# Attention block with residual and layernorm: the softmax reciprocals spread through DRAM, the division taken from PSUM, and a new order of all engines

## The chip, the cores and the metric

The kernel runs on one core of one Trainium2 chip. The metric is the device time in microseconds (us) of the whole launch, all 32 batches in one program; lower is better.

## The reference

`x` is 32 x 256 x 384 (32 batches, 256 rows, 384 columns), `adj` 32 x 256 x 256, all in float32; there are 12 heads of 32 columns.

```python
q, k = x @ Wq.T, x @ Wk.T                      # per head: [32, 12, 256, 32]
v = x @ Wv.T + bv
a = einsum('bnhd,bmhd->bhnm', q, k) * SCALE + adj[:, None]     # [32, 12, 256, 256]
a = where(all(a == 0, axis=-1)[..., None], -inf, a)
a = nan_to_num(softmax(a, axis=-1))            # a row that was all zero gives zero
o = einsum('bhnm,bmhd->bnhd', a, v)            # back to [32, 256, 384]
out = layernorm(x + o @ Wo.T + bo)             # over the 384 columns, eps 1e-5
```

## The kernel before, in words

**Work.** The batches go through a software pipeline, and each of the five instruction streams (TensorE, VectorE, ScalarE, GpSimd and the DMA queue of SyncE) has its own order, written out by hand as a list of calls: `start()` for the first batches, `step(t)` for batches 3 to 29, `end()` for the last. Semaphores alone tie the streams together. A step of TensorE holds work of four batches: `nxt2` (t+2), `nxt` (t+1), `prev` (t-1), `prev2` (t-2).

**A batch.** TensorE projects k and q in three pieces K01, K2Q0 and Q12 (`project_kq`, 18 matmuls each, every float32 product made from three products of split halves `_hi` and `_lo`) into bank_c or bank_b. It projects v in two halves (`project_v`, 9 matmuls each, bank_b). `scores(t, g)` makes the scores of four heads (group g, 0 to 2) in four banks `s_bank`, 24 matmuls. VectorE's `add_bias` adds adj, negates and takes the row's extreme, one instruction per head and half of the rows: 24 in a batch, in 12 units of two. ScalarE's `exps` takes the exponential of a unit and leaves the row sums in `sums`. The unnormalised weights must be transposed. For groups 0 and 1 VectorE transposes them in 32x32 blocks (`square`, 8 in a batch), SyncE stores 1 MB to DRAM (`store_squares`, sq_dram) and loads it in another order (`load_squares`, sq_probT). For group 2, units 8 to 11, TensorE transposes (`transposes`, 4 matmuls a unit, into bank_t) and ScalarE copies out (`copy_probT`). `weigh(t, g)` multiplies v by the weights, 16 matmuls into bank_a, which holds one group at a time, transposed (columns of o on the partitions).

**Division, which the change touches.** `invert` (L1264, VectorE) makes the 24 reciprocals of each row. They stand with rows on the partitions, but the weighed values have rows along the free axis. So GpSimd widens them 32 times (`widen_inv`, L418), and TensorE transposes the wide tile with six matmuls (`spread`, L858), four into bank_c (R0) and two into bank_t (R1). Meanwhile ScalarE copies each weighed group out of bank_a (`save_o`, L576, into o_raw), which frees the bank for the next `weigh`. VectorE multiplies o_raw by the bank of reciprocals (`divide`, L1273, once for groups 0 and 1, once for 2) into o_n, one buffer. `split_o_hi` (ScalarE) and `split_o_lo` (GpSimd) split o_n; `project_y` (9 matmuls each of two halves) applies Wo; VectorE's `residual` and `moments`, GpSimd's `deviation` and ScalarE's `normalise` finish the batch.

**The flag.** `find_zero`, `flag` (one matmul, into the free half of bank_a), `read_flag` (L1240) and `mask` look for rows that are all zero. `mask` loads the flag into a register of VectorE's sequencer (L1248) and branches over its body.

**What may wait.** `weigh` waits until the bank was saved, `scores(t, g)` until `add_bias` has read the four banks of the group before it, and the DMA queue issues strictly in its order, so a wait at its head holds back everything behind it:

```python
def load_squares(t, g):
    sp.wait_ge(sq_stored[g], t.count(DMA, DMA))
    apart(sp)
    after(sp, pv_done[g], t.count(1))
```

Of the kernel before, what the change touches and what calls it, by code (L numbers as in the profile page):

```python
# [13 lines left out]
P = 128  # L14
# [66 lines left out]
def build(nc, x, xT, adj, wqT, wkT, wvT, bv, woT, bo, out):  # L81
    def sb(name, shape, dt=F32):
# [23 lines left out]
    sums = [sb(f"sums{p}", [P, NT, H]) for p in range(2)]  # L106
# [15 lines left out]
    most = sb("most", [P, NT, H])  # L122
    inv = sb("inv", [P, NT, H])
    inv_wide = sb("inv_wide", [P, NT, H, HD])
    o_raw = [sb(f"o_raw{p}", [P, KC, N]) for p in range(2)]
    o_n = sb("o_n", [P, KC, N])
# [19 lines left out]
    bank = {"R0": bank_c, "K01": bank_c, "Q12": bank_c, "PV0": bank_a, "PV1": bank_a, "PV2": bank_a,  # L146
            "K2Q0": bank_b, "V0": bank_b, "V1": bank_b, "Y0": bank_b, "Y1": bank_b}
    t_flat = bank_t[:].rearrange("p k m q -> p (k m q)")
    bank["R1"] = t_flat
    flags_at = bank_a[:, N:N + NT * H]  # L150
# [3 lines left out]
    last_bank = {"R0": s_flat[0], "Y0": s_flat[0], "R1": s_flat[1], "Y1": s_flat[1], "PV1": s_flat[2], "PV2": bank_c[:]}  # L154
# [42 lines left out]
    o_saved = [sem(f"o_saved{g}") for g in range(KC)]  # L197
# [4 lines left out]
    inv_wide_ready = sem("inv_wide_ready")  # L202
    inv_spread = sem("inv_spread")
# [11 lines left out]
    CONSTS = 4  # L215
# [7 lines left out]
    with nc.Block() as block:  # L223

        @block.sync
        def _(sp):
# [32 lines left out]

            def store_out(t):  # L260
# [27 lines left out]
            def start():  # L288
                t0 = Batch(0)
                t1 = Batch(1)  # L290
                t2 = Batch(2)
                t3 = Batch(3)
                t4 = Batch(4)
                load_bias(t1)
                load_xt(t2)
                load_xr(t0)
                store_squares(t0, 0)
                load_xr(t1)
                load_squares(t0, 0)
                load_xt(t3)  # L300
                store_squares(t0, 1)
                load_xt(t4)
                load_squares(t0, 1)
                load_bias(t2)
                store_squares(t1, 0)
                store_squares(t1, 1)
                load_squares(t1, 0)
                load_squares(t1, 1)
                load_bias(t3)
                store_squares(t2, 0)  # L310
                load_squares(t2, 0)
                load_xr(t2)
                store_squares(t2, 1)
                load_bias(t4)
                load_squares(t2, 1)
                store_squares(t3, 0)
                store_out(t0)

            def step(t):
                nxt2 = t.later(2)  # L320
                nxt = t.later(1)
                prev2 = t.later(-2)
                load_xt(nxt2)
                load_bias(nxt2)
                load_squares(t, 0)
                store_squares(t, 1)
                load_squares(t, 1)
                load_xr(t)
                store_squares(nxt, 0)
                store_out(prev2)  # L330

            def end():
                t28 = Batch(28)
                t29 = Batch(29)
                t30 = Batch(30)
                t31 = Batch(31)
                store_squares(t30, 1)
                load_squares(t30, 0)
                load_squares(t30, 1)
                store_squares(t31, 0)  # L340
                load_xr(t30)
                load_squares(t31, 0)
                store_squares(t31, 1)
                store_out(t28)
                load_squares(t31, 1)
                store_out(t29)
# [5 lines left out]
            for c in range(3, 30):  # L352
                step(Batch(c))
# [4 lines left out]
        def _(pool):  # L358
# [3 lines left out]
            pool.wait_ge(const_ready, 3)  # L362
# [41 lines left out]
            def split_o_lo(t, k):  # L404
# [5 lines left out]
                nc.gpsimd.tensor_tensor(o_lo[:, a:b], o_n[:, a:b], o_hi[:, a:b].bitcast(F32), ALU.subtract  # L410
                                        ).then_inc(o_ready, 1)

            def widen_inv(t):
                pool.wait_ge(inv_ready, t.count(1, 1))

                after(pool, inv_spread, t.count(2))
                apart(pool)
                nc.gpsimd.tensor_copy(inv_wide[:], inv[:].unsqueeze(3).to_broadcast([P, NT, H, HD])  # L418
                                      ).then_inc(inv_wide_ready, 1)
# [19 lines left out]
            def start():  # L439
# [9 lines left out]
                split_kq(t0, "Q12")  # L449
                permute_bias(t1)  # L450
                split_kq(t1, "K01")
                split_xt(t2)
                split_kq(t1, "K2Q0")
                split_kq(t1, "Q12")
                split_kq(t2, "K01")
                widen_inv(t0)
                split_kq(t2, "K2Q0")
                split_kq(t2, "Q12")
                permute_bias(t2)
                split_xt(t3)  # L460
                add_bo(t0)
                split_xt(t4)
                split_o_lo(t0, 0)
                split_kq(t3, "K01")
                split_o_lo(t0, 1)
                widen_inv(t1)
                split_kq(t3, "K2Q0")
                permute_bias(t3)
                add_bo(t1)
                split_kq(t3, "Q12")  # L470
                deviation(t0)
                widen_inv(t2)
                split_o_lo(t1, 0)
                split_kq(t4, "K2Q0")

            def step(t):
# [4 lines left out]
                permute_bias(nxt)  # L481
                split_o_lo(prev2, 1)
                split_kq(nxt, "K01")
                add_bo(prev)
                split_xt(nxt2)
                split_kq(nxt, "Q12")
                deviation(prev2)
                split_kq(nxt2, "K2Q0")
# [1066 lines left out]
```

## Time and profile before

| | |
|---|---|
| median of 3 runs | 718.36 us (717.56 to 718.78) |
| profiled execution, its own time | 718.51 us |
| its span, first to last instruction | 716.2 us |
| outside the span | 2.3 us |
| mean granted TensorE clock | 0.997 |

The profile page gives each engine's busy time, the span in 40 slices, and the chain of work that ended last. From its trace come groups of instructions by line, the same chain in order of time, and the instructions of a stretch with what each waited for. A steady batch begins every 21.45 us (K01 at 317.44 and at 338.89).

### The profile page before, as it was taken

What the parts mean: (1) busy time and instruction counts of PE and PEld (TensorE: products, weight loads), DVE (VectorE), ACT (ScalarE), POOL (GpSimd) and SP (SyncE); (2) the same over time, 40 slices, a digit from 0 to 9 for tenths busy, and PEclk for the clock granted to TensorE, in tenths of its full rate; (3) what the DMA queues carried; (4) which work ended last, traced back from release to release, by engine and by line L of the source; (5) the groups of instructions that cost most, each with busy time, mean ns of one, the idle gap of its engine ahead of it and who ended that gap; (6) DMA issues with size and microseconds to landing.
All of it is one profiled execution on the core that took longest, in us unless ns stands there. A gap on an engine that the chain in (4) does not pass through costs nothing.

```text
span 716.2 us, 23143 instructions
## 1 busy us (share of the span) xinstructions
PE 698.7 (98%) x7557; PEld 600.7 (84%) x7557; DVE 600.1 (84%) x2220; ACT 613.8 (86%) x1993; POOL 487.2 (68%) x548
## 2 busy tenths in 40 slices
PE   8999999999999999999999999999999999999895
PEld 8878888888888888888888888888898888888774
DVE  4898988889888889888889888889888889888973
ACT  4889988889988889988888988889888888898882
POOL 4767666677766678766677766678766677766452
PEclk9999999999999999999999999999999999999998
DMA  8475877787777687777787777787777777777672
GB/s 266 152 278 206 300 267 264 252 315 236 263 263 273 241 309 240 265 264 267 251 302 240 262 267 259 252 305 247 257 270 261 262 291 248 255 273 259 248 288 90
DMA packets 84008, 184.61 MB, mean 258 GB/s; under 512 B 4272, under 2 KB 42928, under 8 KB 75696
## 3 DMA queue, kind: packets, MB, share of 16 engines
q1 hardware_dynamic: 83888, 183.12, 72.3%
q8 instruction: 61, 1.00, 0.6%
q14 instruction: 59, 0.48, 0.2%
HBM read 103.42 MB, written 79.69 MB: 256 GB/s over the span
## 4 chain that ended last, share of the span: by engine, by line
PE 85%; DVE 5%; DMA 4%; issue 2%; POOL 2%; ACT 1%; SPq 0%; DVEq 0%; ACTq 0%; POOLq 0%
PE bank_b L787 34%; PE bank_c L787 16%; PE bank_a L877 12%; PE s_bank L836 11%; PE bank_t L847 8%; PE bank_c L858 2%; DVE neg L1192 2%; DMA sq_dram<-w_f 2%; DMA sq_probT<-sq_dram 2%; ACT prob L559 1%; PE bank_t L858 1%; DVE w_f L1209 1%; DMA xt<-in_xT 1%; POOL kq_lo L400 0%; DVE y L1292 0%
## 5 line engine op out<-in xcount | busy, mean ns | idle before, releaser
L559 ACT ACTIVATE prob<-neg,negmax 128x256 f32<-128x256 f32 x768 | 380.3, 500 | 51.8 <-DVE w_f L1209 34.3
L1192 DVE CUSTOM_DVE_ANT_0 neg<-s_bank,bias_sq 128x256 f32<-128x256 f32 x512 | 185.2, 414 | 49.0 <-issue 42.6
L1209 DVE STREAM_TRANSPOSE w_f<-prob 128x512 f32<-128x512 f32 x256 | 173.2, 696 | 0.7 <-ACT prob L559 0.7
L559 ACT ACTIVATION_READ_ACCUMULATOR prob<-neg,negmax 128x1 f32 x768 | 147.7, 192 | 0.0
L400 POOL TENSOR_TENSOR kq_lo<-kq,kq_hi 128x512 fp32r<-128x512 f32 x96 | 125.2, 1304 | 7.7
L398 POOL CAST kq_hi<-kq 128x512 fp32r<-128x512 f32 x96 | 60.2, 627 | 79.3 <-issue 73.9
L787 PE MATMUL bank_c<-xt_hi,w_hi 128*128 128x256 f32 x384 | 111.1, 289 | 1.0 <-DVE w_lo L1171 1.0
L787 PE MATMUL bank_c<-xt_hi,w_lo 128*128 128x256 f32 x384 | 108.3, 282 | 0.0
L787 PE MATMUL bank_c<-xt_lo,w_hi 128*128 128x256 f32 x384 | 108.3, 282 | 0.0
L1192 DVE CUSTOM_DVE_ANT_0 neg<-s_bank,bias 128x256 f32<-128x256 f32 x256 | 91.0, 420 | 15.2 <-PE s_bank L836 15.0
L847 PE MATMUL bank_t<-ident,prob 128*128 128x128 f32 x512 | 80.3, 279 | 0.7 <-ACT probT L569 0.7
L569 ACT ACTIVATE probT<-bank_t 128x512 f32<-128x512 f32 x128 | 75.0, 586 | 3.6 <-PE bank_t L847 2.9
L787 PEld LDWEIGHTS bank_c<-xt_hi,w_hi 128*128 128x128 f32 x384 | 73.0, 190 | 2.1 <-issue 1.7
L410 POOL TENSOR_TENSOR o_lo<-o_n,o_hi 128x512 fp32r<-128x512 f32 (+1 forms) x62 | 63.4, 1025 | 15.4 <-ACT o_hi L584 15.4
L787 PEld LDWEIGHTS bank_c<-xt_hi,w_lo 128*128 128x128 f32 x384 | 73.1, 190 | 0.0
L787 PEld LDWEIGHTS bank_c<-xt_lo,w_hi 128*128 128x128 f32 x384 | 73.1, 190 | 0.0
L877 PE MATMUL bank_a<-sq_probT,v 128*32 128x256 f32 x1008 | 67.5, 385 | 1.2 <-DVE zero_flag L1240 1.0
L787 PE MATMUL bank_b<-w_hi,o_hi 128*128 128x384 f32 x186 | 68.3, 367 | 0.3 <-DVE y L1292 0.3
L787 PE MATMUL bank_b<-w_hi,xt_hi 128*128 128x384 f32 x192 | 67.8, 353 | 0.3 <-ACT kq L542 0.2
L836 PE MATMUL s_bank<-kq_hi 32*128 32x256 f32 x768 | 65.2, 328 | 2.6 <-POOL kq_lo L400 1.3
L836 PEld LDWEIGHTS s_bank<-kq_hi 32*128 32x128 f32 x768 | 37.3, 183 | 34.4 <-issue 33.3
L847 PEld LDWEIGHTS bank_t<-ident,prob 128*128 128x128 f32 x512 | 56.5, 140 | 10.7 <-issue 1.6
(88 smaller groups left out, 1794.1 us busy)
## 6 DMA issues: line engine op xcount, KB each, us to landing
sq_dram<-w_f SPq DMA_DIRECT2D x64, 1024.0 KB, 4.5
sq_probT<-sq_dram SPq DMA_DIRECT2D x64, 1024.0 KB, 5.6
xt<-in_xT SPq DMA_DIRECT2D x32, 384.0 KB, 4.5
xr<-in_x SPq DMA_DIRECT2D x32, 384.0 KB, 6.2
out_y<-y_out SPq DMA_DIRECT2D x31, 384.0 KB, 3.0
bias<-in_adj SPq DMA_DIRECT2D x32, 256.0 KB, 3.2
w_f<-in_wkT SPq DMA_DIRECT2D x3, 192.0 KB, 4.5
w_f<-in_wqT SPq DMA_DIRECT2D x3, 192.0 KB, 5.0
```

The source lines that it names most:

```text
L398: nc.gpsimd.tensor_copy(kq_hi[t.p][:, a:a + 2, :], kq[:, a:a + 2, :]).then_inc(kq_hi_ready[name], 1)
L400: nc.gpsimd.tensor_tensor(kq_lo[t.p][:, a:a + 2, :], kq[:, a:a + 2, :], kq_hi[t.p][:, a:a + 2, :].bitcast(F32), ALU.subtract).then_inc(kq_ ...
L410: nc.gpsimd.tensor_tensor(o_lo[:, a:b], o_n[:, a:b], o_hi[:, a:b].bitcast(F32), ALU.subtract).then_inc(o_ready, 1)
L559: nc.scalar.activation(prob[:, u % PROB_RING, k], neg[:, h, w.c], ACT.Exp, scale=-1.0, bias=negmax[t.p][:, w.c, h:h + 1], accum_out=sums[t ...
L569: nc.scalar.activation(probT[:, a:a + PAIR, :, P * w.c:P * (w.c + 1)], bank_t[:], ACT.Copy).then_inc(probT_act, 1)
L787: last = nc.tensor.matmul(ps, w_pair[a](k), m_pair[b](k), start=(k == 0 and e == 0), stop=(k == KC - 1 and e == 2))
L836: last = nc.tensor.matmul(s_bank[j][:, c, :], a[t.p][rows, KC + g, P * c:P * (c + 1)], b[t.p][rows, g, :], start=(e == 0), stop=(e == 2))
L847: last = nc.tensor.transpose(bank_t[:, k, m, :], prob[:, u % PROB_RING, k, P * m:P * (m + 1)], ident[:])
L858: last = nc.tensor.transpose(bank_at(t, f"R{k}")[:, at:at + P], inv_wide[:, c, JH * g:JH * (g + 1), :].rearrange("p h d -> p (h d)"), iden ...
L877: last = nc.tensor.matmul(bank_at(t, f"PV{g}")[HD * j:HD * (j + 1), 0:N], v[t.p][:, m, HD * h:HD * (h + 1)], weights, start=(m == 0), stop ...
L1192: nc.vector.tensor_tensor_reduce(out=neg[:, h, w.c], in0=s_bank[h % JH][:, w.c, :], in1=by[t.p][:, w.c, :], scale=-1.0, scalar=BIG, op0=AL ...
L1209: nc.vector.transpose(sq_stage[w.g][:, :, a:a + PAIR, :, w.c].rearrange("p b h m s -> p (h m) b s"), prob[:, u % PROB_RING].rearrange("p k ...
```

## The change

Four things, and every order anew:

- `widen_inv` and `spread` are gone, and with them inv_wide and the two banks R0 and R1. VectorE now transposes the small tile of reciprocals itself in 32x32 blocks (`turn_inv`), SyncE stores it to DRAM (`store_inv`, 16 KB) and loads it with every row repeated on 32 partitions (`load_inv`, 384 KB, into one of two buffers inv_all).
- `save_o` and o_raw are gone. `divide` is called for each of the three groups and reads bank_a itself; `weigh` waits for the divide before it (o_n_ready) in place of o_saved. o_n has two buffers.
- The flag matmul writes bank_t; `sums` is laid out so that the transposed rows come in the order of the load.
- `step` now covers batches 3 to 28.

```diff
-            def widen_inv(t):
-                pool.wait_ge(inv_ready, t.count(1, 1))
...
-                nc.gpsimd.tensor_copy(inv_wide[:], inv[:].unsqueeze(3).to_broadcast([P, NT, H, HD])
-            def save_o(t, g):
-                act.wait_ge(pv_done[g], t.count(1, 1))
...
-            def spread(t, k):
...
+            def store_inv(t):
+                sp.wait_ge(inv_turned, t.count(1, 1))
...
+                after(sp, inv_loaded[t.p], t.loads() - DMA)
+                sp.dma_start(inv_dram[t.p].rearrange("k b r -> b k r"),
+                             inv_t[:]).then_inc(inv_stored[t.p], DMA)
+            def load_inv(t):
+                sp.wait_ge(inv_stored[t.p], t.loads())
...
+                after(sp, o_n_ready, t.count(KC, -KC))
+                sp.dma_start(inv_all[t.p][:].rearrange("p g n -> p (g n)"),
+                             inv_dram[t.p][0:JH * KC * NT].rearrange("(j k) b r -> j (k b r)", j=JH).unsqueeze(1)
+                             .to_broadcast([JH, HD, KC * N])).then_inc(inv_loaded[t.p], DMA)
...
             def invert(t):
                 dve.wait_ge(prob_ready, t.count(H * NT, H * NT))
...
+                nc.vector.reciprocal(inv[:, 0:H * NT], sums[t.p][:].rearrange("p j g c -> p (j g c)")
+                                     ).then_inc(inv_ready, 1)
+            def turn_inv(t):
+                dve.wait_ge(inv_ready, t.count(1, 1))
...
+                nc.vector.transpose(inv_t[:], inv[:]).then_inc(inv_turned, 1)
+            def divide(t, g):
+                dve.wait_ge(pv_done[g], t.count(1, 1))
+                if g == 0:
+                    dve.wait_ge(inv_loaded[t.p], t.loads())
+                    after(dve, o_ready, t.count(2, -2))
+                    apart(dve)
+                nc.vector.tensor_tensor(o_n[t.p][:, g, :], bank_at(t, f"PV{g}")[:, 0:N], inv_all[t.p][:, g, :],
                                         ALU.mult).then_inc(o_n_ready, 1)
```

The order of a step on TensorE, T8 standing for `transposes` of unit 8, S for `scores`, W for `weigh`, V and Y for halves of `project_v` and `project_y`, R for `spread`:

```text
before: K01(t+1) V1(t) S2(t) W1(t-1) R0(t-1) Y0(t-2) W2(t-1) S0(t+1) T8(t) Y1(t-2) flag(t) R1(t-1)
        Q12(t+1) T9(t) K2Q0(t+2) T10(t) W0(t) S1(t+1) T11(t) V0(t+1)
now:    Q12(t+1) T11(t-1) S2(t) W0(t-1) Y0(t-2) K01(t+2) Y1(t-2) flag(t) S0(t+1) W1(t-1) K2Q0(t+2)
        W2(t-1) T8(t) V0(t+1) S1(t+1) T9(t) V1(t+1) T10(t)
```

VectorE's step now (a number after add_bias or square is the unit): divide 2 of t-2, add_bias 4 5 6, invert and turn_inv of t-1, square 0, add_bias 7, square 1, save_v 1, square 2, add_bias 8 9, square 3, add_bias 10, residual 0 of t-2, add_bias 11, find_zero, divide 0 of t-1, square 4 5 6, read_flag, residual 1, square 7, mask, divide 1 of t-1, then add_bias 0 to 3 of t+1 among the two moments, and save_v 0 of t+1.

SyncE's queue, one steady batch before, with the waits of each transfer (the number behind L is the line in each kernel):

```order
154 L231 DMA xt<-in_xT 128x3x256 [waits xt_ready]
155 L236 DMA bias<-in_adj 128x2x256 [waits neg_ready]
156 L257 DMA sq_probT<-sq_dram 128x4x512 [waits sq_stored0,pv_done0]
157 L248 DMA sq_dram<-w_f 128x2048 [waits squared,sq_loaded1]
158 L257 DMA sq_probT<-sq_dram 128x4x512 [waits sq_stored1,pv_done1]
159 L241 DMA xr<-in_x 128x2x384 [waits y_saved]
160 L248 DMA sq_dram<-w_f 128x2048 [waits squared,sq_loaded0]
161 L268 DMA out_y<-y_out 128x2x384 [waits y_ready]
```

The same queue with the change:

```order
150 L235 DMA xt<-in_xT 128x3x256 [waits xt_ready]
151 L252 DMA sq_dram<-w_f 128x2048 [waits squared,sq_loaded1]
152 L245 DMA xr<-in_x 128x2x384 [waits y_saved]
153 L261 DMA sq_probT<-sq_dram 128x4x512 [waits sq_stored0,pv_done0]
154 L240 DMA bias<-in_adj 128x2x256 [waits neg_ready]
155 L269 DMA inv_dram<-inv_t 4x32x32 [waits inv_turned,inv_loaded0]
156 L277 DMA inv_all<-inv_dram 128x1x768 [waits inv_stored0,o_n_ready]
157 L261 DMA sq_probT<-sq_dram 128x4x512 [waits sq_stored1,pv_done1]
158 L289 DMA out_y<-y_out 128x2x384 [waits y_ready]
```

The load of group 1's squares (row 157) now stands behind the store and the load of the reciprocals, and so behind `turn_inv`.

TensorE around `weigh` of group 1, before (bank_c<-ident,inv_wide is `spread`):

```order
1519 L836 MATMUL s_bank<-kq_hi,kq_lo 128x256 x4
1520 L877 MATMUL bank_a<-sq_probT,v 32x256 [waits sq_loaded1,v_saved,o_saved0]
1521 L877 MATMUL bank_a<-sq_probT,v 32x256 x7
1522 L858 MATMUL bank_c<-ident,inv_wide 128x128 [waits inv_wide_ready,kq_saved_K01]
1523 L858 MATMUL bank_c<-ident,inv_wide 128x128 x3
1524 L787 MATMUL bank_b<-w_hi,o_hi 128x384 [waits o_ready,v_saved]
```

The same place with the change:

```order
1541 L878 MATMUL s_bank<-kq_hi,kq_lo 128x256 x4
1542 L907 MATMUL bank_a<-sq_probT,v 32x256 [waits sq_loaded1,v_saved,o_n_ready]
1543 L907 MATMUL bank_a<-sq_probT,v 32x256 x7
1544 L829 MATMUL bank_b<-xt_hi,w_hi 128x256 [waits xt_ready,y_saved]
```

`spread` is gone behind it, and the bank's release now comes from VectorE.

VectorE where the reciprocals are made, with the change (each pair of ISA rows is one `add_bias` instruction; these are the last of units 4 to 6):

```order
768 L1226 ISA neg,negmax<-s_bank,bias_sq 128x256 [waits scored,prob_ready]
769 L1226 ISA negmax 128x1
770 L1226 ISA neg,negmax<-s_bank,bias_sq 128x256
771 L1226 ISA negmax 128x1
772 L1303 RECIPROCAL inv<-sums 128x24 [waits inv_turned,const_ready,prob_ready]
773 L1312 STREAM_TRANSPOSE inv_t<-inv 128x32 [waits inv_ready,inv_stored0]
774 L1243 STREAM_TRANSPOSE w_f<-prob 128x4x4x32 [waits prob_ready,sq_stored0]
```

Before, `invert` of the same batch stood between units 1 and 2 of the next batch; now it and the new `turn_inv` follow that batch's unit 6.

## Rows read from the trace of the kernel before

**Rows 1.** The page: busy time, and the chain that ended last by engine
```profile
PE 698.7 (98%) x7557; PEld 600.7 (84%) x7557; DVE 600.1 (84%) x2220; ACT 613.8 (86%) x1993; POOL 487.2 (68%) x548
...
PE 85%; DVE 5%; DMA 4%; issue 2%; POOL 2%; ACT 1%; SPq 0%; DVEq 0%; ACTq 0%; POOLq 0%
```
**Rows 2.** Busy us (and instructions) by stage: PE, PEld, DVE, ACT, POOL, PEclk, DMA, GB/s
```profile
300.00:400.00 100.00, 100.00 (x1101) 85.59 (x1093) 85.10 (x322) 87.91 (x291) 69.66 (x76) 1.00 0.76 265
```
**Rows 3.** The chain in order of time, one steady batch: start, us, what
```profile
319.59 1.57 PE bank_b L787 x9
...
323.07 0.59 PE bank_c L858 x4
...
329.36 0.27 PE bank_t L858 x2
...
332.21 2.16 PE bank_b L787 x18
334.37 0.44 PE bank_t L847 x4
334.81 1.00 PE bank_a L877 x16
335.81 0.91 PE s_bank L836 x24
336.72 0.59 PE bank_t L847 x4
...
342.61 0.91 PE s_bank L836 x21
```
**Rows 4.** Groups by line: us busy, mean ns, idle before and its releaser
```profile
L576 ACT ACTIVATE o_raw<-bank_a 128x256 f32<-128x256 f32 x94 | 34.8, 371 | 1.2 <-PE bank_a L877 1.1
...
L1273 DVE TENSOR_TENSOR o_n<-o_raw,bank_t 128x256 f32<-128x256 f32 x31 | 12.7, 408 | 0.8 <-PE bank_t L858 0.8
...
L1264 DVE RECIPROCAL inv<-sums 128x24 f32<-128x24 f32 x32 | 9.5, 297 | 0.7 <-ACT prob L559 0.6
```
**Rows 5.** VectorE in order of time: start, us, instruction, idle before it
```profile
342.65 0.56 DVE L1229 TENSOR_TENSOR v<-bank_b,bv_all 128x384 f32<-128x384 f32 x1 [0.56 <-PE bank_b L787]
343.76 0.42 DVE L1192 CUSTOM_DVE_ANT_0 neg<-s_bank,bias 128x256 f32<-128x256 f32 x1 [0.55 <-PE s_bank L836]
344.11 0.08 DVE L1192 DVE_READ_ACCUMULATOR2_ANT negmax<- 128x1 f32 x1
...
348.62 0.64 DVE L1273 TENSOR_TENSOR o_n<-o_raw,bank_c 128x512 f32<-128x512 f32 x1
...
349.90 0.18 DVE L1302 BATCH_NORM_AGGREGATE meanvar<-stats 128x2 f32<-128x6 f32 x1 [0.17 <-DVE stats L1297]
...
353.33 0.42 DVE L1192 CUSTOM_DVE_ANT_0 neg<-s_bank,bias_sq 128x256 f32<-128x256 f32 x1 [1.54 <-issue]
```
**Rows 6.** The register load of the flag, line 1248: ns min/median/max
```profile
L1248 DVEq TENSOR_LOAD <-zero_flag x32: 303/888/1171, 35.6 to 694.4; - x32
```
**Rows 7.** The DMA view, issues by line: KB each, median us to landing
```profile
sq_probT<-sq_dram SPq DMA_DIRECT2D x64, 1024.0 KB, 5.6
...
xr<-in_x SPq DMA_DIRECT2D x32, 384.0 KB, 6.2
...
out_y<-y_out SPq DMA_DIRECT2D x2, 192.0 KB, 1.9
```
**Rows 8.** The DMA queue in order of time: issue of two loads
```profile
355.50 0.36 SPq L257 DMA_DIRECT2D sq_probT<-sq_dram  x1
355.90 0.51 SPq L241 DMA_DIRECT2D xr<-in_x  x1
```
**Rows 9.** The last load of squares, and TensorE's wait for it
```profile
693.71 0.36 SPq L257 DMA_DIRECT2D sq_probT<-sq_dram  x1
...
699.34 1.07 PE L877 MATMUL s_bank<-sq_probT,v 128*32 128x256 f32 x16 [1.08 <-DMA sq_probT<-sq_dram]
```
**Rows 10.** VectorE near the end: the last reciprocals
```profile
695.06 0.30 DVE L1264 RECIPROCAL inv<-sums 128x24 f32<-128x24 f32 x1 [0.60 <-ACT prob L559]
```

More of the change, by code:

```diff
@@ L121, in build @@
     zero_flag = sb("zero_flag", [1, 1], I32)
[L122 to L126, printed above, removed]
+    most = sb("most", [P, H, NT])
+    empty = sb("empty", [P, JH, KC, NT])
+    inv = sb("inv", [P, SQ])
+    inv_t = sb("inv_t", [P, SQ])
+    inv_dram = [nc.dram_tensor(f"inv_dram{p}", (SQ, BLOCKS, SQ), F32, kind="Internal").ap() for p in range(2)]
+    inv_all = [sb(f"inv_all{p}", [P, KC, N]) for p in range(2)]
+    o_n = [sb(f"o_n{p}", [P, KC, N]) for p in range(2)]
     o_hi = sb("o_hi", [P, KC, N], F32R)
@@ L351, in _ @@
             start()
-            for c in range(3, 30):
+            for c in range(3, 29):
                 step(Batch(c))
@@ L515, in _ @@
             start()
-            for c in range(3, 30):
+            for c in range(3, 29):
                 step(Batch(c))
@@ new lines, in end @@
+                flag(t29)
+                pe.wait_ge(y_saved, t27.count(NT, 1))
+                project_y(t27, 1)
+                pe.wait_ge(o_n_ready, t28.count(KC, 1))
+                weigh(t28, 1)
+                pe.wait_ge(flag_read, t29.count(1, 1))
+                transposes(t29, 8)
+                scores(t30, 0)
+                pe.wait_ge(o_n_ready, t28.count(KC, 2))
+                weigh(t28, 2)
+                pe.wait_ge(y_saved, t27.count(NT, 2))
+                project_kq(t31, "K2Q0")
@@ L1072, in end @@
+                copied(t29, 8)
+                transposes(t29, 9)
+                scores(t30, 1)
+                copied(t29, 9)
+                transposes(t29, 10)
+                pe.wait_ge(kq_saved["K2Q0"], t31.count(1, 1))
+                project_v(t30, 0)
+                copied(t29, 10)
+                transposes(t29, 11)
                 scores(t30, 2)
-                pe.wait_ge(o_saved[0], t29.count(1, 1))
-                weigh(t29, 1)
+                pe.wait_ge(o_n_ready, t28.count(KC, 3))
@@ L1075, in end @@
+                weigh(t29, 0)
                 pe.wait_ge(v_saved, t30.count(NT, 1))
                 project_v(t30, 1)
+                pe.wait_ge(v_saved, t30.count(NT, 2))
+                project_y(t28, 0)
+                copied(t29, 11)
+                flag(t30)
+                pe.wait_ge(o_n_ready, t29.count(KC, 1))
+                weigh(t29, 1)
+                scores(t31, 0)
+                pe.wait_ge(flag_read, t30.count(1, 1))
+                transposes(t30, 8)
                 pe.wait_ge(kq_saved["K01"], t31.count(1, 1))
```

753 lines of the change are left out of this document (398 added, 355 removed).

## The prediction

> **What bounds the kernel now.** I read the page first. TensorE is busy 98% of the span, and 85% of the chain that ended last lies on it; the other engines are busy 68 to 86% [rows 1]. The table by stage says where: in the middle of the run TensorE is busy 100.00 of 100 us at full clock [rows 2]. So a steady batch costs what TensorE's instructions cost, 21.45 us, and each other engine only has to be on time. The chain in order of time gives the price of each piece there [rows 3]. The groups by line, VectorE in order of time and the DMA rows [rows 4 to 10] then show how much room there is for work that moves elsewhere.
>
> **TensorE, removed.** `spread` takes 0.59 us (four transposes) and 0.27 us (two) of the chain in each batch [rows 3]: 0.86 us, wholly on the path, the largest term. The rest of TensorE's work is unchanged, but its neighbours change. Four transposes cost 0.44 us between products of kind K and 0.59 us between scores and a half of V or Y [rows 3]; before, two of the four units paid each. Now units 8 and 9 stand ahead of a V half, unit 10 behind one and unit 11 ahead of scores, so up to 0.15 more for one or two of them; I take 0.1 us. TensorE's own floor becomes 21.45 - 0.86 + 0.1 = 20.7 us.
>
> **ScalarE and GpSimd, removed.** Three copies of 0.37 us a batch go from ScalarE [rows 4], and GpSimd loses the widening; ScalarE was busy 88% [rows 2] and falls to about 87% of the shorter period. I cost both at nothing, since neither was or becomes the bound. They are freer to be on time, which is worth nothing while TensorE has no wait.
>
> **VectorE, added.** It must now carry what TensorE gives up. In a period of 21.45 us it waited 0.56 us for v and 0.55 us for scores, so 20.3 us were taken, among them the 1.54 us before the first `neg` behind the flag [rows 5]. Changes: three divides of about 0.41 us, as the one on 256 columns [rows 4], in place of one of 0.64 [rows 5] and one of 0.41; as each instruction starts 0.07 us before the one ahead has ended (0.35 from start to start for a `neg` of 0.42 [rows 5]), that is +0.1. `turn_inv` handles 32 columns: no row has it, the nearest are a reciprocal on 24 columns, 0.30 [rows 4], and the `meanvar` of 0.18, which also waits 0.17 for the instruction ahead, as `turn_inv` must for `invert` [rows 5]; I take 0.3 for both together. Against this, `mask` now stands behind `square` 7 and not behind `read_flag`. The flag's register load took 888 ns in the median but 303 ns at best [rows 6], and can partly run beside the square. So VectorE needs between 20.3 + 0.4 - 0.6 = 20.1 and 20.7 us, that is as much as TensorE's floor at the upper end. VectorE was late for nothing before; now it has 0 to 0.6 us of slack in a loop with TensorE at three places (the scores banks, the v halves, bank_a). I take 0.2 us a batch of waits for this: between 0, the lower end, and the 1.1 us of its own two waits if they stayed in full on top of the 20.1 (21.2 us).
>
> The Trainium skill ("DMA: Bandwidth & Descriptors", section on latency) puts the floor of such a register load at about 600 ns; by it 0.3 of the 0.6 us would be saved. The trace's shortest, 303 ns, is below that floor [rows 6], so the trace decides.
>
> **The wait that the change adds.** bank_a is now released by a divide, and group 0's divide waits for the reciprocals to have gone to DRAM and back. The queue order matters more: the load of group 1's squares stands behind `store_inv` and `load_inv`, both of which wait at the queue's head. This closes a loop of exactly one batch: `weigh` 1, K2Q0, `weigh` 2, T8, V0, S1 on TensorE, `add_bias` 4 to 6, `invert`, `turn_inv` on VectorE, store, load, load of squares, next `weigh` 1. Its price:
> - TensorE's six pieces: 1.00 + 2.16 + 1.00 + 0.59 + 1.57 + 0.91 = 7.23 us [rows 3].
> - scores to the first `neg`: 343.76 against 342.61 + 0.91 = 343.52, 0.24 us [rows 3, 5].
> - six `add_bias` instructions at 0.35: 2.1; reciprocal, wait and turn: 0.30 + 0.17 + 0.2 = 0.67 [rows 4, 5]. `turn_inv` ends 10.24 us after `weigh` 1 began.
> - store: 16 KB in pieces of 128 B. The smallest store seen, 192 KB, landed after 1.9 us [rows 7]; less would be the fixed part alone, and the 4.5 us of a 1 MB store would be the other end. I take 1.9, the nearest size, and 0.1 for the queue to react.
> - the two loads, 384 KB and 1 MB right behind it: the trace has this pair in the other order, issued 0.4 us apart, the second landing 6.2 us later, so 6.6 us for both [rows 7, 8]; the 1 MB load alone takes 5.6 [rows 7]. I take 6.6 and 0.15 to TensorE's start.
>
> Together 19.0 us, 1.7 under the floor: hidden, in my forecast. That cover is the thinnest in the plan: the loop sets the period as soon as store and loads need over 10.3 us together, and makes the kernel slower from about 11.1 us.
>
> DMA traffic: 5.6 MB a batch grow by 0.4 MB, at a share of 0.76 [rows 2], so about 0.85 of the shorter batch; the average leaves room.
>
> **Start and end.** Near the end nothing hides the way through DRAM. The last load of squares was issued at 693.71 and TensorE had waited 1.08 us for it at 699.34 [rows 9]. Now it waits for the last `turn_inv`, behind a reciprocal of 695.06 [rows 10]: 695.06 + 0.67 + 0.1 + an issue of 0.36 = 696.2, so 2.5 us later. The last `project_y` of batch 30 now comes ahead of that wait and takes 1.6 us of it. I charge 1.5 us (0 to 3). The start has no such place: nothing.
>
> **Sum.** A period of 20.9 us saves 0.55 us in each of 32 batches, 17.6 us. From the profiled execution's own 718.51 us: 718.51 - 17.6 + 1.5 = 702.4, and since it lies 0.15 us above the median of the runs, the same to the digit that counts: **702.5 us**. Its own range, periods of 20.7 to 21.1: 695 to 709.
>
> **Rivals.**
> 1. *The loop through DRAM sets the period, below the old one.* `load_inv` reads four rows of 3 KB, each repeated for 32 partitions; every load in the trace has 128 in the outermost place. If the transfer were dealt out by those four rows, four DMA engines would carry 96 KB each and not sixteen 24 KB. A busy engine moves 265 / 0.76 / 16 = 21.8 GB/s [rows 2], so 72 KB more take 3.4 us on those four; if they are faster while the others idle, perhaps 2. The squares' load queues behind. For it: the odd pattern, the thin cover. Against it: no row shows such a split. With 2 us more, the loop is 21.0 to 21.2 us, and 32 x 0.35 = 11.2 us less plus 1.5 to 3 at the end gives about **709 us**.
> 2. *The same loop, above the old period.* With the full 3.4 us on four engines, or with 3 us instead of 1.9 for a store of 128-byte pieces and 2 more on the loads, the loop is 22.1 to 22.4, at 21.45 + 0.1 it decides against the change. At 21.9 on average: 718.5 + 29 x 0.45 + 3 = about **734 us**. Place: TensorE idle ahead of `weigh` 1 in every batch.
> 3. *VectorE becomes the bound.* The register load stays at 0.9 us and the two waits stay: 21.1 to 21.2 us a batch, **710 us**, with TensorE's idle time ahead of scores.
> That the change doesn't do what it says is excluded: the orders show no transpose of inv_wide left.
>
> The Trainium skill ("DMA: Bandwidth & Descriptors", sections on why a DMA increments its semaphore by 16 and rules for kernel authors) says that a DMA uses the largest number of engines up to 16 that divides the outermost dimension on both sides, so that an outermost four confines it to four engines. By that rule rivals 1 and 2 would hold with all their price, on the store too; no row here bears on it, as all DMAs of the trace have 128 outermost.
>
> **How the numbers follow.** Forecast 0.42; rival 1 0.22; rival 2 0.29; rival 3 0.07. The range 693 to 735 reaches from just under the forecast's own best end into rival 2 to its middle, where a tenth and more stays outside. About 0.2% (1.4 us) is what a measurement of this kernel can tell from no change. Faster: all of the forecast, nearly all of rivals 1 and 3, 0.68; the same 0.06, where rivals 1 and 2 meet; slower 0.26.
>
> **What would show it.** Right: TensorE busy over 99% in the middle, a batch every 20.7 to 21.1 us, `load_inv` landing in 3 to 5 us, squares' load in under 7, no wait of `weigh` for a DMA. Rival 1 or 2: `load_inv` over 5.5 us, sq_probT at 8 us or more for one of the two loads, TensorE waiting for "DMA sq_probT<-sq_dram" or for o_n in every batch. Rival 3: waits of s_bank for negmax. The gap behind the flag should fall from 1.54 us to under 1.2. The forecast is wrong if the period is above 21.2 us.

## The result, and the profile after

The kernel with the change takes 843.03 us (median of 4 runs, 836.69 to 859.63), the kernel before 718.49 us beside it (717.56 to 718.78). The ratio is 1.1707, with a 95% interval of 1.1633 to 1.178. The forecast was 702.5 us, with a range of 693 to 735: wrong in sign and far outside. The profiled execution is the slowest of the four (859.63 us, span 857.8 us, mean granted clock 0.918 against 0.929 to 0.942 in the others) and counts as a slow run, so the ratio leaves it out and its waits may be longer than those of the median run. Its 26 batches from 64.36 to 741.19 us take 26.0 us on average, 23.8 to 27.7; the one taken apart below takes 27.3. The page of the kernel after, busy time and the chain that ended last, against [rows 1]:

```profile
PE 739.0 (86%) x7365; PEld 627.7 (73%) x7365; DVE 614.6 (72%) x2284; ACT 590.2 (69%) x1897; POOL 462.4 (54%) x517
...
DMA 48%; PE 32%; DVE 10%; issue 5%; SPq 2%; POOL 1%; ACT 0%; DVEq 0%; ACTq 0%; POOLq 0%
DMA sq_probT<-sq_dram 35%; PE bank_b L829 16%; PE bank_a L907 9%; DMA inv_dram<-inv_t 7%; DVE neg L1226 6%; PE s_bank L878 3%; DMA sq_dram<-w_f 3%; DMA inv_all<-inv_dram 3%; PE bank_t L889 2%; SPq L277 2%; DVE negmax L1226 1%; DVE inv_t L1312 1%; DVE inv L1303 1%; DVE w_f L1243 1%; DMA xt<-in_xT 1%
```

TensorE has fallen from 98% to 86% of a longer span, and the chain, 85% TensorE before, is now 48% DMA. One transfer leads it: the load of squares. TensorE's busy time rose by 40 us although the change took six transposes a batch away from it. The table by stage gives a first hint (columns as in [rows 2]):

```profile
300.00:400.00 100.00, 86.92 (x844) 74.21 (x843) 70.81 (x267) 67.19 (x220) 52.91 (x60) 0.90 0.75 241
...
415.00:417.00 2.00, 2.00 (x17) 1.01 (x8) 0.82 (x3) 0.93 (x4) 0.00 (x0) 0.50 0.67 265
421.00:428.00 7.00, 7.00 (x72) 6.32 (x65) 4.26 (x19) 5.49 (x18) 4.57 (x7) 1.00 0.48 176
```

In the middle of the run TensorE is busy 87 of 100 us, at a mean granted clock of 0.90. The chain in order of time over one batch, as in [rows 3], shows a loop that closes on itself:

```profile
400.19 1.94 DMA inv_dram<-inv_t
...
402.22 0.54 SPq L277
...
402.87 11.35 DMA sq_probT<-sq_dram
...
414.36 1.93 PE bank_a L907 x16
416.29 4.04 PE bank_b L829 x18
420.33 1.00 PE bank_a L907 x16
421.33 0.59 PE bank_t L889 x4
421.92 1.57 PE bank_b L829 x9
423.49 0.94 PE s_bank L878 x21
...
427.18 0.23 DVE inv_t L1312
...
427.49 1.95 DMA inv_dram<-inv_t
```

From one store of the reciprocals (400.19) to the next (427.49) the chain has no gap: store 1.94 us, issue of the reciprocals' load 0.54, then 11.35 us from the issue of the squares' load until it has landed, then `weigh` 1 (bank_a), K2Q0, `weigh` 2, T, V0 and S on TensorE, the last `neg` instructions, `inv` and `inv_t` on VectorE. It is the loop which the prediction wrote out and held to be hidden. Two engines stand still for it. TensorE in order of time, then VectorE, the idle time before an instruction in brackets:

```profile
414.36 1.93 PE L907 MATMUL bank_a<-sq_probT,v 128*32 128x256 f32 x16 [3.67 <-DMA sq_probT<-sq_dram]
```

```profile
411.80 0.42 DVE L1321 TENSOR_TENSOR o_n<-bank_a,inv_all 128x256 f32<-128x256 f32 x1 [3.71 <-DMA inv_all<-inv_dram]
```

So the reciprocals' load, issued at 402.22, had landed just before 411.80, about 9.5 us after its issue, and the squares' load behind it about 12 us after that same issue. Over the whole run, the waits:

```profile
DVE o_n L1321 <- DMA inv_all<-inv_dram: 88.3, 27, 4.2
PE bank_a L907 <- DMA sq_probT<-sq_dram: 86.2, 28, 4.6
```

The DMA view, which has the same columns as [rows 7]:

```profile
sq_probT<-sq_dram SPq DMA_DIRECT2D x64, 1024.0 KB, 8.1
...
inv_all<-inv_dram SPq DMA_DIRECT2D x32, 384.0 KB
...
inv_dram<-inv_t SPq DMA_DIRECT2D x32, 16.0 KB
```

The squares' load went from 5.6 to 8.1 us in the median (it has two a batch; 11.35 is the one behind the reciprocals). For the two DMAs whose outermost dimension is four, this view gives no landing time at all; their times are read from who waited for them. One thing did come out as hoped, the register load of the flag, against [rows 6]:

```profile
L1282 DVEq TENSOR_LOAD <-zero_flag x32: 302/304/892, 34.1 to 823.8; - x32
```

The median fell from 888 to 304 ns.

The clock accounts for most of what TensorE's own pieces lost. Over 421 to 428 us the granted clock is 1.00; at 415 to 417, right after TensorE has stood still for 3.67 us, it is 0.50, that is the 1.2 GHz level. `weigh` 1 took 1.93 us and K2Q0 4.04, against 1.00 and 2.16 in [rows 3]: 0.93 + 1.88 = 2.8 us more in this batch, inside the very loop that had made TensorE wait. About 0.25 of it is not the clock: in the new order the two pieces take 1.07 and 2.35 us at full clock as well. That is seen in the batches where the clock did not fall, in the same chain:

```profile
654.02 1.07 PE bank_a L907 x16
655.09 2.35 PE bank_b L829 x18
```

The fall does not come in every batch. Of the 26 with `weigh` 1 between 102 and 755 us, three ran both pieces at full clock, behind waits of 3.00, 2.96 and 2.69 us; the other 23 were slower by 1.4 to 2.7 us, one of them behind a wait of 2.35. The clock's mean price is 1.8 us a batch.

### The profile page after: what moved, and what is told of

It is laid out like the page before. It is cut to its first block, busy times and chain, and to the rows that moved or that the text cites. A ratio compares the mean times of both kernels' runs of the same rounds, so it can differ in the third digit from the quotient of the medians.

```text
span 857.8 us, 22669 instructions
## 1 busy us (share of the span) xinstructions
PE 739.0 (86%) x7365; PEld 627.7 (73%) x7365; DVE 614.6 (72%) x2284; ACT 590.2 (69%) x1897; POOL 462.4 (54%) x517
## 4 chain that ended last, share of the span: by engine, by line
DMA 48%; PE 32%; DVE 10%; issue 5%; SPq 2%; POOL 1%; ACT 0%; DVEq 0%; ACTq 0%; POOLq 0%
DMA sq_probT<-sq_dram 35%; PE bank_b L829 16%; PE bank_a L907 9%; DMA inv_dram<-inv_t 7%; DVE neg L1226 6%; PE s_bank L878 3%; DMA sq_dram<-w_f 3%; DMA inv_all<-inv_dram 3%; PE bank_t L889 2%; SPq L277 2%; DVE negmax L1226 1%; DVE inv_t L1312 1%; DVE inv L1303 1%; DVE w_f L1243 1%; DMA xt<-in_xT 1%
## 5 line engine op out<-in xcount | busy, mean ns | idle before, releaser
L907 PE MATMUL bank_a<-sq_probT,v 128*32 128x256 f32 x1008 | 83.3, 456 | 93.6 <-DMA sq_probT<-sq_dram 86.2
L1321 DVE TENSOR_TENSOR o_n<-bank_a,inv_all 128x256 f32<-128x256 f32 x94 | 39.3, 418 | 123.6 <-DMA inv_all<-inv_dram 88.3
L907 PEld LDWEIGHTS bank_a<-sq_probT,v 128*32 128x32 f32 x1008 | 31.6, 121 | 117.2 <-issue 98.7
L1226 DVE CUSTOM_DVE_ANT_0 neg<-s_bank,bias 128x256 f32<-128x256 f32 x256 | 94.1, 415 | 8.0 <-PE s_bank L878 7.9
L584 ACT ACTIVATE kq<-bank_b 128x512 f32<-128x512 f32 x32 | 19.1, 596 | 97.1 <-PE bank_b L829 96.2
L889 PEld LDWEIGHTS bank_t<-ident,prob 128*128 128x128 f32 x512 | 58.3, 142 | 21.0 <-issue 13.4
L829 PE MATMUL bank_b<-xt_hi,w_hi 128*128 128x256 f32 x192 | 73.1, 381 | 0.3 <-POOL xt_lo L435 0.3
```

The source lines that it names most:

```text
L829: last = nc.tensor.matmul(ps, w_pair[a](k), m_pair[b](k), start=(k == 0 and e == 0), stop=(k == KC - 1 and e == 2))
L889: last = nc.tensor.transpose(bank_t[:, k, m, :], prob[:, u % PROB_RING, k, P * m:P * (m + 1)], ident[:])
L907: last = nc.tensor.matmul(bank_at(t, f"PV{g}")[HD * j:HD * (j + 1), 0:N], v[t.p][:, m, HD * h:HD * (h + 1)], weights, start=(m == 0), stop ...
L1226: nc.vector.tensor_tensor_reduce(out=neg[:, h, w.c], in0=s_bank[h % JH][:, w.c, :], in1=by[t.p][:, w.c, :], scale=-1.0, scalar=BIG, op0=AL ...
L1321: nc.vector.tensor_tensor(o_n[t.p][:, g, :], bank_at(t, f"PV{g}")[:, 0:N], inv_all[t.p][:, g, :], ALU.mult).then_inc(o_n_ready, 1)
```

## The experiments

Theory A: the reciprocals' load is confined to four of the sixteen DMA engines by its outermost dimension of four (rival 1's and 2's mechanism), and the squares' load queues behind it. Against it stood: that reading the same four rows 32 times is slow; that any load of 384 KB at this place, behind a round trip that blocks the queue, costs as much; and that VectorE or the new order of the work costs something by itself.

**e1_four_loads.** The same bytes and the same repeated rows, as four loads into 32 partitions each, with 32 outermost (semaphore counts follow, not shown):

```diff
-   sp.dma_start(inv_all[t.p][:].rearrange("p g n -> p (g n)"),
-                inv_dram[t.p][0:JH * KC * NT].rearrange("(j k) b r -> j (k b r)", j=JH).unsqueeze(1)
-                .to_broadcast([JH, HD, KC * N])).then_inc(inv_loaded[t.p], DMA)
+   for j in range(JH):
+       sp.dma_start(inv_all[t.p][HD * j:HD * (j + 1)].rearrange("p g n -> p (g n)"),
+                    inv_dram[t.p][KC * NT * j:KC * NT * (j + 1)].rearrange("k b r -> (k b r)").unsqueeze(0)
+                    .to_broadcast([HD, KC * N])).then_inc(inv_loaded[t.p], DMA)
```

> The load of the reciprocals is issued as four loads of 32 partitions each, one per row of 3 KB, so that the outermost place of each holds 32 and not 4; bytes, sources and repeats stay. Theory A (four in the outermost place confine the transfer to four DMA engines, and the squares' load queues behind it there): the reciprocals land about 4 us after the last of the four issues, the squares' load in about 6.5 us in place of 11.4, the loop closes at about 21.1 us and the kernel takes about 710 us (700 to 730). Theory B (128 reads of the same few KB of DRAM are slow however they are dealt): the reciprocals still land after some 9 us and the kernel stays at 820 to 860 us. Theory C (the store, the load and the place in the queue alone, at any speed of the load): over 780 us.

Measured: 726.61 us (722.42 to 733.2, 8 runs), ratio 1.012 [1.0065, 1.0174]; mean granted clock 0.995. The DMA view and the queue in order of time:

```profile
sq_probT<-sq_dram SPq DMA_DIRECT2D x64, 1024.0 KB, 6.9
...
inv_all<-inv_dram SPq DMA_DIRECT2D x128, 96.0 KB, 2.4
```

```profile
363.19 0.52 SPq L269 DMA_DIRECT2D inv_dram<-inv_t  x1
365.20 1.72 SPq L278 DMA_DIRECT2D inv_all<-inv_dram  x4
367.04 0.38 SPq L261 DMA_DIRECT2D sq_probT<-sq_dram  x1
```

116 of the 125 us are gone, and each quarter of the load lands in 2.4 us. What it costs now is where it stands: the squares' load is issued 367.04 - 363.19 = 3.85 us after the store, and lands 6.9 us later. With the 10.24 us of the prediction for the part on TensorE and VectorE, and 0.15, that is an estimated loop of 21.1 us, just about the period; TensorE still waits 12.3 us in all for this load, in 17 places. The time lies in Theory A's 700 to 730 us, but 17 us above its 710. Theories B (820 us and more) and C (over 780) are out.

**e3_rows128.** The same 384 KB as one load of 128 distinct rows of x, with 128 outermost (so it divides by other values, here and in e5):

```diff
-                inv_dram[t.p][0:JH * KC * NT].rearrange("(j k) b r -> j (k b r)", j=JH).unsqueeze(1)
-                .to_broadcast([JH, HD, KC * N])).then_inc(inv_loaded[t.p], DMA)
+                x[t.c].rearrange("(p a) d -> p (a d)", p=P)).then_inc(inv_loaded[t.p], DMA)
```

> The load of the same 384 KB comes from 128 different rows of x (so the division is by other values; the rest of the work is unchanged), with 128 in the outermost place. Theory A and theory B both: it lands in 4 to 5 us, the squares' load in about 6.5, kernel 700 to 720 us. Theory C: over 780 us.

Measured: 714.47 us (709.59 to 718.21, 8 runs), ratio 0.9931 [0.988, 0.9981]. The DMA view:

```profile
sq_probT<-sq_dram SPq DMA_DIRECT2D x64, 1024.0 KB, 7.2
...
inv_all<-in_x SPq DMA_DIRECT2D x32, 384.0 KB, 3.2
```

So a load of that size at that place, in one issue, is no loss at all: the size alone is not it. It still leaves two differences, the repeated rows and the outermost dimension.

**e5_four_by_32.** Again distinct rows of x, but dealt out as four times 32:

```diff
+   c0 = min(t.c, B - JH)
...
+                x[c0:c0 + JH, 0:2 * HD, :].rearrange("j (q a) d -> j q (a d)", a=2)
+                ).then_inc(inv_loaded[t.p], DMA)
```

> The load of the same 384 KB comes from 128 different rows of x, but as four blocks of 32 rows that lie apart, so that 4 stands in the outermost place again (the division is by other values). Theory A (confined by the outermost 4): as slow as the changed kernel, 800 to 860 us, squares' load about 10 to 11 us behind it. Theory B (slow because the same rows are read again and again): 700 to 720 us.

Measured: 881.35 us (878.96 to 883.75, 2 runs), ratio 1.2238 [1.2035, 1.2442], granted clock 0.90. The waits are those of the change:

```profile
PE bank_a L908 <- DMA sq_probT<-sq_dram: 97.7, 28, 4.7
DVE o_n L1322 <- DMA inv_all<-in_x: 93.6, 27, 4.6
```

No row is read twice in one load here, and the loss is larger still, above Theory A's 800 to 860 us. Part of that is the clock: `weigh` 1 takes 1.93 us or more, as at the lower level, in 23 of the 26 batches from 104 us on, in the change in 14 of 26; why stays open. Repetition is refuted as the cause. Between this kernel and e3_rows128, with as many bytes from the same tensor, stands the outermost dimension, 4 against 128, and with it that the source is four blocks in different batches of x and not one; no run separates these two, but in e1_four_loads and the change the source is the same.

**e4_no_trip.** The new orders and divides alone. It leaves out the store and the load of the reciprocals; the divides use values that are loaded once.

```diff
+            for p in range(2):
+                sp.dma_start(inv_all[p][:].rearrange("p g n -> p (g n)"),
+                             x[p].rearrange("(p a) d -> p (a d)", p=P)).then_inc(inv_loaded[p], DMA)
...
-                store_inv(t)
-                load_inv(t)
                 load_squares(t, 1)
```

> No store and no load of reciprocals: both tiles of reciprocals are filled once at the start from x, everything else keeps its order (it leaves out the spread of the reciprocals). What is left is the floor of the new order. All theories: no wait of TensorE in a steady batch beyond 0.2 us, a batch every 20.7 to 20.9 us, 692 to 702 us. If it is over 715 us, VectorE is a bound of its own.

Measured: 707.11 us (706.29 to 707.94, 2 runs), ratio 0.9819 [0.9666, 0.9972]. The middle stage, and pieces of the chain in order of time:

```profile
300.00:400.00 100.00, 100.00 (x1104) 85.67 (x1103) 89.79 (x338) 84.98 (x278) 67.83 (x76) 1.00 0.81 271
```

```profile
302.81 2.34 PE bank_b L818 x18
...
316.35 1.79 PE bank_b L818 x9
...
321.87 0.03 PE bank_t L903
...
342.86 0.03 PE bank_t L903
```

TensorE is the bound again at full clock, and the same piece comes back after 342.86 - 321.87 = 20.99 us: that is the floor, not 20.7, and the time is 5 us above the 692 to 702 that all theories expected. The two pieces that follow a `weigh` are longer than their kind: K2Q0 2.34 where the other pieces of 18 matmuls take 2.15, a Y half 1.79 where others take 1.57 to 1.59. Together 0.4 us for two new neighbours, where the prediction had allowed 0.1.

**e6_both** and **e7_order_only.** The squares' load is moved ahead of the store of the reciprocals everywhere, so that nothing that TensorE needs first stands behind the round trip; e6 on top of e1's four loads, e7 on the change as it is.

```diff
-                store_inv(t)
-                load_inv(t)
-                load_squares(t, 1)
+                load_squares(t, 1)
+                store_inv(t)
+                load_inv(t)
```

> The four loads of the run before, and the load of group 1's squares moved ahead of the store of the reciprocals in the queue, so that it no longer waits for turn_inv. Theory A (what is left of the loop runs over the squares' load): TensorE's 10.9 us of waits for that load go, the loop now closes over the divide alone (10.2 + 0.1 + 1.95 + 2.2 of issues + 2.4 landing + 0.5 = 17.4 us), a batch every 21.0 us, 706 to 711 us. Rival (the store's and the loads' own traffic and issue time hold the rest of the queue back): 715 us or more, with TensorE waiting for some other transfer.

> The changed kernel with only the queue's order mended: the load of group 1's squares ahead of the store of the reciprocals; the load of the reciprocals stays one transfer with four in the outermost place. Theory A (confined to four engines, about 9.5 us from issue to landing): the squares land in time, but the divide that frees bank_a still waits for the reciprocals: 10.2 + 0.1 + 1.95 + 9.5 + 0.5 = about 22.3 us for the loop, and the clock's fall on top where TensorE stands still: 740 to 790 us. Rival (the place in the queue was the whole cause): under 715 us.

Measured: e6 727.61 us (722.75 to 730.44, 6 runs), ratio 1.0105 [1.0064, 1.0146]; e7 851.98 us (850.38 to 853.58, 2 runs), ratio 1.1848 [1.1782, 1.1913]. e6 came out at its rival's 715 us or more, though TensorE waits there for VectorE (8.8 us for `residual`, 4.3 for the flag) and not for a transfer itself. e7 came out at neither: its rival, that the place in the queue was the whole cause (under 715 us), is refuted, and Theory A's 740 to 790 us was too low by 60, though what it describes is there: `weigh` waits for the divide (60.0 us in 24 places) and the divide for the reciprocals (111.2 us in 27). e7's chain in order of time:

```profile
301.51 1.98 DMA inv_dram<-inv_t
303.58 7.91 DMA inv_all<-inv_dram
...
324.00 4.29 DMA inv_dram<-inv_t
...
328.38 8.78 DMA inv_all<-inv_dram
```

With the squares' load out of the way the loop closes over the divide instead: the reciprocals' load takes 7.9 to 8.8 us in these two batches, and the store up to 4.3 when squares are on their way before it. So the queue order of the squares' load is not the main cause; whichever transfer is asked for, the confined load delays it.

e7 also lets one see the confined load by itself, since nothing else is issued in the 2 us behind it; in the first of them nothing moves. The columns are those of [rows 2], so the last two are the DMA share of sixteen engines and GB/s; the first two lines are from e7, the third from e1, where the four loads of 32 partitions are alone until 367.04:

```profile
303.60:304.60 1.00, 1.00 (x29) 0.87 (x32) 0.85 (x2) 1.00 (x4) 0.93 (x1) 1.00 0.00 0
304.70:305.60 0.90, 0.90 (x17) 0.38 (x10) 0.82 (x5) 0.90 (x4) 0.90 (x2) 1.00 0.23 63
```

```profile
366.10:367.00 0.90, 0.90 (x23) 0.42 (x16) 0.57 (x4) 0.90 (x5) 0.90 (x1) 1.00 0.58 212
```

A share of 0.23 is the busy time of 3.7 engines in sixteen; in three more batches it is 0.20 to 0.23, at 44 to 48 GB/s. Four engines, busy nearly all the time, would show just that; the same bytes as four loads show 9.3 engines and 212 GB/s, so the load's confinement is seen and not only inferred from times.

e6 shows the price of this order with a fast load: from 100 to 400 us TensorE is busy over 99.5 of each 100 us, but the store stands behind 1 MB (4.5 to 6.5 us in the late batches), and SyncE holds its queue until it has landed. Its middle is good, its last batches are not:

```profile
300.00:400.00 100.00, 99.55 (x1074) 86.01 (x1073) 90.54 (x336) 87.07 (x285) 70.51 (x77) 1.00 0.86 289
...
650.00:700.00 50.00, 43.16 (x450) 34.24 (x449) 42.94 (x159) 43.06 (x146) 23.14 (x29) 0.97 0.77 262
```

**e8_before_four** and **e9_before_rows.** The kernel before with an extra load of 256 KB a batch for which no one waits, issued ahead of the load of squares 1; dealt out as 4 times 32 in e8, as 128 rows in e9.

```diff
+            def load_extra(t):
+                ...
+                sp.dma_start(w_space[:, 2 * AREA:2 * AREA + 2 * N], x[c0:c0 + JH, 0:2 * HD, :].rearrange("j (q a) d -> j q (a d)", a=2)[:, :, 0:2 * N]
+                             ).then_inc(extra_in, DMA)
...
                 store_squares(t, 1)
+                load_extra(t)
                 load_squares(t, 1)
```

> The kernel before, with an additional load of 256 KB in each steady batch that nothing waits for, right ahead of the load of group 1's squares, with four in the outermost place. Theory A (64 KB more on each of four engines): the squares' load behind it lands some 4 us later (9 to 10 us from issue in place of 5.6), more than the 3.8 us of room that it has, so TensorE waits: 725 to 760 us. Theory B (only repeated rows of DRAM are slow): 718 us.

> As the run with four in the outermost place, but the same 256 KB with 128 in the outermost place (16 KB on each of sixteen engines). All theories: the squares' load lands under 7 us, the room of 3.8 us covers it: 717 to 721 us.

Measured: e8 717.83 us (716.96 to 719.53, 8 runs), ratio 0.9984 [0.9961, 1.0008]; e9 718.21 us (717.54 to 720.58, 8 runs), ratio 0.9997 [0.9971, 1.0022]. The 725 us and more expected of e8 were a miss. The queue of e8 in order of time:

```profile
351.43 0.56 SPq L266 DMA_DIRECT2D w_f<-in_x  x1
355.63 0.36 SPq L258 DMA_DIRECT2D sq_probT<-sq_dram  x1
```

The squares' load is issued 4.2 us after the confined one, since it waits for the store of its squares (issued at 350.97) to land; the squares' loads land 5.9 us after their issue in the median (5.6 before). The confined one was then still running: the DMA share from 355 to 356 us is 0.24 in e8 (first row) and 0.00 in the kernel before (second row):

```profile
355.00:356.00 1.00, 1.00 (x10) 1.00 (x10) 1.00 (x6) 1.00 (x5) 1.00 (x1) 1.00 0.24 78
355.00:356.00 1.00, 1.00 (x11) 1.00 (x10) 1.00 (x8) 1.00 (x5) 1.00 (x1) 1.00 0.00 0
```

In the change the distance was 402.87 - 402.22 = 0.65 us, and the load behind took 11.35 us. So a confined load delays those who wait for it and those queued right behind it; this one, with time around it and room behind it, cost nothing that the times show. How much of the difference is the distance and how much the size (256 against 384 KB) these two runs do not separate.

**e10_squares_between** and **e11_four_loads_again.** e1's loop of 21.1 us says what to move: the store first, since it is small and early, then the squares' load while the store is on its way, then the four loads. e10 does this to e1's kernel, e11 is e1's kernel again.

```diff
                 store_inv(t)
-                load_inv(t)
                 load_squares(t, 1)
+                load_inv(t)
```

> The reciprocals' load stays split into four loads of 32 partitions, as in e1_four_loads, and in the batches 1 to 28 the load of squares 1 is issued between the store and the load of the reciprocals, where it waits neither for the store to land nor for four issues. Theory A (what is left over the kernel without the trip, 727 against 707 us, is mostly the second squares' load, which stood behind the store's 1.94 us and four issues of 0.46): TensorE's wait for sq_probT falls from 10.9 us to under 3, the divide does not wait for inv_all, and the time comes to 712 to 720 us. Rival (the load of the reciprocals then queues behind 1 MB and the SP queue is held for just as long: the loop closes over the divide, as when both were put behind the squares): VectorE waits for inv_all by 10 us or more in all and the time stays at 723 to 731 us.

> The kernel of e1_four_loads once more, on the same chip as e10_squares_between, so that the two can be set side by side: 722 to 733 us by both theories, TensorE's wait for sq_probT 8 to 14 us.

Measured on one chip: e10 714.22 us (712.57 to 715.95, 5 runs), ratio 0.9937 [0.9913, 0.9961]; e11 727.13 us (723.86 to 731.07, 5 runs), ratio 1.0136 [1.0105, 1.0167]. e10 is 0.6% faster than the kernel before, and far faster than the change. Its queue, waits, start and middle:

```profile
400.82 0.53 SPq L269 DMA_DIRECT2D inv_dram<-inv_t  x1
401.47 0.41 SPq L261 DMA_DIRECT2D sq_probT<-sq_dram  x1
403.51 1.73 SPq L278 DMA_DIRECT2D inv_all<-inv_dram  x4
```

```profile
DVE o_n L1322 <- DMA inv_all<-inv_dram: 14.3, 20, 2.4
```

```profile
0.00:100.00 100.00, 91.35 (x997) 80.81 (x997) 77.57 (x285) 74.77 (x233) 60.31 (x65) 1.00 0.72 242
300.00:400.00 100.00, 100.00 (x1072) 86.31 (x1073) 90.33 (x340) 85.43 (x281) 68.16 (x77) 1.00 0.86 296
```

The squares' load is issued 0.65 us after the store, not 3.85. TensorE's wait for it fell from 11.7 us in e11 to 1.7 us, one wait in the last batch. Theory A's time came out, but not all of its picture: the divide does wait for the reciprocals, 14.3 us in 20 places, as the rival had it. These waits fall into VectorE's slack and cost TensorE little, 0 to 0.5 us in each 100 from 100 to 600 us. What is left over e4_no_trip's 707 us lies mostly at the start (TensorE busy 91.35 of the first 100 us, 95.96 in e4_no_trip) and in the last batches; I did not try to win it.

## Why the prediction was wrong

**The step that failed** is the term "the two loads": 6.6 us for the pair, by the row of two loads with 128 outermost. In the batch shown, from the issue of the first (402.22) to TensorE's start (414.36) it is 12.1 us, against 6.6 + 0.15: 5.4 us short. The squares' load takes 10.8 us on average over the 26 batches and 11.35 here, so the mean shortfall is 4.9. With it fell the conclusion "19.0 us, 1.7 under the floor: hidden". The prediction named the mechanism, as rivals 1 and 2, gave its price as at most 3.4 us and held "no row shows such a split" against it. With that price the pair would have taken 10.0 us; from the issue of the first to the landing of the second it was 12.0. The prediction counted the reciprocals' 72 KB more on four engines, but not what else those engines carry: 96 KB of reciprocals, 64 KB of the squares, and 64 KB more if the store of squares issued at 405.64 gets in between. An estimate from [rows 2] (21.8 GB/s for a busy engine) gives 4.5 + 3.0 = 7.5 us, or 10.5 with the store, and with the 1.9 us of a small transfer 9.4 to 12.4 us. Nor did the confined load reach that rate at its start: e7's rows have 44 to 63 GB/s, where four engines at 21.8 would move 87. How the four share their time was not tried.

**The clock.** The prediction priced TensorE's pieces of the loop at full clock throughout, 7.23 us; that the clock could fall was not foreseen at all. Together with the loads, the batch shown is 19.0 + 5.4 + 2.8 = 27.2 us, against a measured 27.3. On average it is 19.0 + 4.9 + 1.8 for the clock + 0.25 for the two pieces in their new places = 25.9, against 26.0. I had let the rival's loop end at 22.4 us. A loop well over 21 us makes TensorE wait, the clock was at its lower level behind 23 of 26 such waits, and that lengthens the same loop. No run holds the waits and changes only the clock, so its share is read from the rows and not from an experiment. In e1_four_loads, whose loop is 21.1 us, the waits are short (12.3 us in 17) and the mean clock of the profiled execution is 0.995.

The Trainium skill ("DMA: Bandwidth & Descriptors", sections on why a DMA increments its semaphore by 16 and rules for kernel authors) states that the engines used are the largest number up to 16 that divides the outermost dimension on both sides. The runs agree: e5_four_by_32 against e3_rows128 (881 against 714 us), e1_four_loads against the change (727 against 843), and the share of 0.20 to 0.23 while the confined load runs alone. The profile gives only the mean over sixteen, so which engines these are is not shown. The rule stood in the prediction; rivals 1 and 2 had 0.51 of the chance together, and a price that was too small.

**TensorE, removed.** Right for the 0.86 us; the neighbours cost 0.4 and not 0.1 (e4_no_trip), so the floor is 20.99 and not 20.7. The 0.1 was for `transposes`, the 0.4 came from the pieces behind `weigh`. The forecast's period of 20.9, with 0.2 us of waits for VectorE on top of 20.7, was near it by luck: two errors against each other.

**VectorE.** Sized too high. In the batch of e4_no_trip from 321.87 us it waits 0.39 + 0.19 + 0.22 + 0.35 = 1.15 us for TensorE, so 19.8 of 20.99 us are taken, against 20.1 to 20.7 predicted. TensorE is busy 100 of 100 us there, and rival 3 is out. The register load fell to 304 ns: right; at the place of the old gap of 1.54 us VectorE idles for 0.39 us in e4_no_trip. **ScalarE and GpSimd** at nothing: right, though the 87% for ScalarE was a slip: 87.91% of 21.45 us less three copies of 0.37 is 85% of 20.9, and e4_no_trip has 84.98.

**The rest of the loop.** `weigh` 1 to the end of `turn_inv` at full clock: 10.24 us predicted, in e4_no_trip 322.80 to 333.18 = 10.38. The store: 1.9 predicted, 1.94 measured, although it too has four outermost; with 16 KB that costs nothing visible. That this cover was the thinnest in the plan, and that the loop sets the period once store and loads need over 10.3 us, was right: they needed 14 in the batch shown.

**The end.** +1.5 us was for the squares' load; in the change the last load of reciprocals, issued behind it at 832.51, takes 10.43 us on the chain, in e10_squares_between 5.48. The term left this load out and was too small; by how much, no run separates.

## What to carry to other kernels

Look at the outermost dimension of both sides of every DMA, most of all for one that broadcasts few rows to many partitions, and split it so that it no longer has only a few in the outermost place: here 32 in place of 4 was worth 116 us of 125, and 128 (e3_rows128) did no worse; nothing between 4 and 32 was run. When a new transfer enters a loop that spans one iteration, write the loop's sum with every queue position in it, and if it comes within a few us of the period, price the stall with the slower clock that may follow it (23 times in 26 here). In a queue that waits at its head, put the small, early store first, then whatever others need at once, and the load that depends on the store last (714 against 727 us for that move alone, e10 against e11).

## What the runs showed of the hardware that was not expected

- A load of 384 KB with four outermost landed about 9.5 us after its issue, with the squares' load behind it at 12; with 128 outermost 3.2 us, and as four loads of 96 KB with 32 outermost 2.4 us each, although these read the same 3 KB 32 times.
- Alone on the queue, the load with four outermost kept 0.20 to 0.23 of the sixteen DMA engines busy, the same bytes as four loads 0.58.
- The same kind of load with 256 KB and 4.2 us before the next one cost nothing, although it was still running when the next was issued (0.9984 [0.9961, 1.0008]).
- After a stall of 3.67 us the granted clock was 0.50 at 415 to 417 us and was back at 1.00 some 6 us after TensorE's start. Waits of 2.4 to 4.6 us were followed by slower pieces in 23 of 26 batches; behind waits of 2.69, 2.96 and 3.00 us they ran at full clock.
- A product of 128 x 128 weights that follows a `weigh` with its 32-column weights took 0.2 us longer as a group than one that follows its own kind (1.79 against 1.59, 2.34 against 2.15).
- VectorE's register load of the flag took 302 ns at the least and 304 in the median once other work stood between the reduction and it; before, 888.
